# Two heads in 32 array columns: the value product of a pruned attention kernel

## The reference

```python
q, k, v = heads(xn @ w_attn.T + b_attn)            # 16 heads of 8 columns
att = q @ k.T / sqrt(8), causal
S = relu(att[:, 0]), column 0 and diagonal set to 0  # head 0 only
FF = cumsum over the rows of S, shifted by one row
att = att - FF[:, None]
keep = the 102 smallest FF of a row (fewer in early rows), and the diagonal
att = where(keep, att, -inf)
y = softmax(att) @ v
out_attn = y @ w_proj.T + b_proj
# ffn: top 2 of 8 experts by a softmax gate; each expert relu(xn@wi.T + bi + lora) @ wo.T + bo
```

## Time and profile before

| what | us |
|---|---|
| median of 3 executions (660.19 to 662.8) | 660.26 |
| the profiled execution | 663.88 |
| its span, first to last instruction | 661.9 |
| busy: TensorE, VectorE, GpSimd, ScalarE | 561.8, 505.3, 445.7, 378.0 |
| one batch of 44 slots, undisturbed | 74.2 |
| start of the first score | 48.1 |
| mean granted clock of TensorE, share of full | 0.958 |

### The profile page before, as it was taken

One profiled execution on the slowest core, in us unless ns is written; L12 is line 12 of the kernel. 1 busy time (PEld: TensorE's weight loads), 2 busy tenths in 40 slices (PEclk: granted clock), 3 DMA queues, 4 the chain that ended last, 5 costly groups with the idle time before them and its releaser, 6 DMA issues.

```text
span 661.9 us, 16486 instructions
## 1 busy us (share of the span) xinstructions
PE 561.8 (85%) x5434; PEld 382.5 (58%) x5434; DVE 505.3 (76%) x1832; ACT 378.0 (57%) x815; POOL 445.7 (67%) x756
## 2 busy tenths in 40 slices
PE   4636879989888899889998898989998899899994
PEld 1413555766466665656566565666566565776583
DVE  7679798667997679857897769867897769975351
ACT  3452776565765565754756566664756556455542
POOL 7506948696578746796478955798478956496451
PEclk9656999999999899989999999999999999999998
DMA  4152052134001520025100430025000430000000
GB/s 100 25 63 27 1 63 35 30 47 61 1 17 28 65 30 1 18 47 63 11 18 17 60 45 1 17 43 70 9 1 18 60 44 1 2 14 5 1 2 17
DMA packets 30068, 19.56 MB, mean 30 GB/s; under 512 B 6089, under 2 KB 29856, under 8 KB 29984
## 3 DMA queue, kind: packets, MB, share of 16 engines
q1 hardware_dynamic: 29984, 18.50, 19.5%
HBM read 3.22 MB, written 2.10 MB: 8 GB/s over the span
## 4 chain that ended last, share of the span: by engine, by line
PE 41%; DVE 19%; POOL 15%; issue 11%; ACT 7%; SPq 4%; DMA 1%; DVEq 1%; ACTq 0%; POOLq 0%
PE ps_t L923 10%; POOL ar L549 9%; PE ps_o L942 9%; PE ps_s L910 6%; PE ps_m L855 4%; SPq L407 4%; DVE ar L1330 4%; ACT work L648 2%; PE ps_m L851 2%; DVE work L1150 2%; PE ps_m L867 2%; ACT pr L734 2%; POOL hsum L563 1%; PE ps_m L873 1%; PE ps_m L885 1%
## 5 line engine op out<-in xcount | busy, mean ns | idle before, releaser
L549 POOL TENSOR_SCALAR ar<-ar,mx 128x512 f32<-128x512 f32 (+3 forms) x512 | 280.2, 561 | 171.4 <-DVE mx L1330 165.1
L734 ACT ACTIVATE pr<-ps_t 128x512 f32<-128x512 f32 (+1 forms) x352 | 192.4, 558 | 80.9 <-PE ps_t L923 78.8
L1330 DVE CUSTOM_DVE_ANT_0 ar<-ps_s,mask 128x256 f32<-128x256 f32 (+2 forms) x384 | 202.9, 550 | 33.2 <-PE ps_s L910 32.3
L923 PE MATMUL ps_t<-ident,ar 128*128 128x128 f32 x1280 | 202.6, 277 | 16.5 <-POOL ar L549 11.0
L923 PEld LDWEIGHTS ps_t<-ident,ar 128*128 128x128 f32 x1280 | 156.2, 142 | 57.2 <-POOL ar L549 27.4
L910 PE MATMUL ps_s<-ks,qs 96*128 96x512 bf16 (+3 forms) x512 | 130.4, 307 | 11.7 <-DVE mx L1327 6.0
L942 PE MATMUL ps_o<-pr,va 128*32 128x128 f32 x2560 | 98.8, 282 | 7.6 <-ACT pr L734 6.1
L942 PEld LDWEIGHTS ps_o<-pr,va 128*32 128x32 f32 x2560 | 63.4, 111 | 48.5 <-ACT pr L734 31.2
L910 PEld LDWEIGHTS ps_s<-ks,qs 96*128 96x128 bf16 x512 | 43.1, 99 | 56.5 <-issue 27.1
L719 ACT ACTIVATE h<-ps_m,bi_col 128x512 f32<-128x512 f32 x64 | 43.9, 687 | 54.9 <-PE ps_m L855 54.2
L855 PE MATMUL ps_m<-zm,b_t 128*128 128x512 f32 x128 | 67.7, 610 | 8.7 <-ACT h L719 8.7
(11 more groups left out here) (227 smaller groups left out, 772.1 us busy)
## 6 DMA issues: line engine op xcount, KB each, us to landing
qs<-parts SPq DMA_DIRECT2D x42, 128.0 KB
ks<-parts SPq DMA_DIRECT2D x42, 128.0 KB
xs<-in_L_attn_x SPq DMA_DIRECT2D x8, 256.0 KB, 3.0
out<-res SPq DMA_DIRECT2D x8, 192.0 KB, 2.0
first_heads<-parts SPq DMA_DIRECT2D x72, 8.0 KB
qs<-parts SPq DMA_DIRECT2D x12, 64.0 KB
ks<-parts SPq DMA_DIRECT2D x12, 64.0 KB
out<-res SPq DMA_DIRECT2D x8, 64.0 KB, 10.5
```

The lines of the kernel that those rows point to most:

```text
L549: nc.gpsimd.tensor_scalar(col, col, -1.0, mx[:, t % NA_RING, j:j + 1], ALU.mult, ALU.add)\
L734: nc.scalar.activation(pr[:, u % NP_RING, 0:w], ps_t[u % NT_RING][:, 0:w], ACT.Exp, scale=-1.0)\
L923: last = nc.tensor.transpose(ps_t[u % NT_RING][:, P * j:P * j + P], ar[:, u % NA_RING, P * j:P * j + P], ident[:, :])
L1330: nc.vector.tensor_tensor_reduce(out=ar[:, t % NA_RING, w * j:w * j + w], in0=ps_s[t % NS_RING][:, w * j:w * j + w], in1=mask[:, k % 2, OF ...
```

## The change

The value product puts two heads into 32 array columns, 16 for each. va gets a layout by pairs of heads (PAIR = 41 columns: v of the even head and a one, filler, nine zeros, filler, v of the odd head and a one). The even head's matmul takes 32 columns from the start of the pair, so that its own rows are 0 to 8 and zeros fall on rows 16 to 24; the odd head's takes 32 columns from 16 on and is accumulated into the same place, its rows being 16 to 24. ORDER arranges the heads so that groups 0 and 1 (2 and 3) hold the even and the odd heads of the same pairs. A row block then needs 256 columns of ps_o, and two row blocks share the bank. out_t is copied at slots 16 and 48 only, ot and yt have two jobs per batch in place of four (at 19 and 50, 22 and 52), each for two row blocks, and proj0 and proj1 now take two row blocks each; their slots and all others stay. va is filled by four copies per v job, since even and odd heads and the two row blocks are copied apart, and GpSimd fills the zeros with eight more fills at the start. The tile s0 goes, and its data is kept in the tile work, so that its writer waits for masks of the batch before.

```diff
@@ -47,7 +47,10 @@
...
-OW = 512 // NH
+OW = 32
+HALF_OW = OW // 2
+PAIR = 41
+OUT_COLS = HALF_OW * NH
@@ -73,6 +76,8 @@
...
+ORDER = [8 * (i // 8) + 2 * (i % 4) + i % 8 // 4 for i in range(NH)]
@@ -89,8 +94,8 @@
...
-OT_AT, YT_AT, PROJ_AT = (12, 19, 36, 50), (17, 22, 39, 52), (40, 55)
-ATT_JOBS = [(f"ot{a}", OT_AT[a], "dve") for a in range(NA)] + [(f"yt{a}", YT_AT[a], "act") for a in range(NA)] + \
+OT_AT, YT_AT, PROJ_AT = (19, 50), (22, 52), (40, 55)
+ATT_JOBS = [(f"ot{a}", OT_AT[a], "dve") for a in range(2)] + [(f"yt{a}", YT_AT[a], "act") for a in range(2)] + \
@@ -244,11 +249,17 @@
...
-        va = sb("va", [P, 2, NA, (NH - 1) * VW + OW])
-        s0 = sb("s0", [P, FOFF[NA]])
+        va = sb("va", [P, 2, NA, NH // 2 * PAIR + VW])
...
+        s0_place = ((0, 0), (1, 0), (2, 0), (1, 3 * P))
+        def s0(j, lo, hi):
+            row, at = s0_place[j]
+            return work[:, row, at + lo:at + hi]
@@ -287,13 +298,13 @@
...
-        bias_part = hsum[0:1, 0:3, :].rearrange("o f t -> o (f t)").bitcast(BF16)[:, 0:6 * (NA - 1) * C]\
-            .rearrange("o (j q a c) -> o j q a c", j=2, q=3, a=NA - 1)
+        bias_part = hsum[0:1, 0:3, :].rearrange("o f t -> o (f t)").bitcast(BF16)[:, 0:12 * C]\
+            .rearrange("o (j q a c) -> o j q a c", j=2, q=3, a=2)
...
-        rec = sb("rec", [P, NH])
+        rec = sb("rec", [P, 2 * NH])
@@ -475,6 +486,8 @@
...
+                    for p in range(NH // 2):
+                        link(nc.gpsimd.memset(va[:, :, :, PAIR * p + HALF_OW:PAIR * p + HALF_OW + VW], 0.0))
@@ -689,11 +702,11 @@
...
-                                    act.wait_ge(scanned, NA * (n - 1) + j + 1)
+                                    act.wait_ge(mask_done, NA * (n - 1) + s0_place[j][0] + 1)
...
-                                nc.scalar.activation(s0[:, FOFF[j]:FOFF[j] + w], m[:, 0:w], ACT.Relu,
+                                nc.scalar.activation(s0(j, 0, w), m[:, 0:w], ACT.Relu,
@@ -703,8 +716,12 @@
...
-                                copy(va[:, into(n), both, 0:NH * VW].rearrange("p a (h d) -> p a h d", d=VW)[:, :, :, 0:HD],
-                                     m3[:, :, 0:P].rearrange("p a (h d) -> p a h d", d=HD), name, n, False)
+                                for i, a in enumerate(half):
+                                    for s in range(2):
+                                        copy(va[:, into(n), a, 0:NH // 2 * PAIR]
+                                             .rearrange("p (h d) -> p h d", d=PAIR)[:, :, OW * s:OW * s + HD],
+                                             m3[:, i, 0:P].rearrange("p (h s d) -> p h s d", s=2, d=HD)[:, :, s, :],
+                                             name, n, False)
@@ -720,9 +737,9 @@
...
-                                if n >= 1 and a in (0, 3):
-                                    wait_full(act, ("proj0", "proj1")[a == 3], n - 1)
-                                copy(yt[:, a, :], m[:, 0:P], name, n)
+                                if n >= 1:
+                                    wait_full(act, f"proj{a}", n - 1)
+                                copy(yt[:, 2 * a:2 * a + 2, :].rearrange("p a t -> p (a t)"), m[:, 0:2 * P], name, n)
@@ -734,12 +751,12 @@
...
-                            for a in range(NA):
+                            for a in (1, 3):
...
-                                    if NA * kk + a >= 1:
-                                        wait_full(act, f"ot{(a + 3) % NA}", kk - (a < 1))
+                                    if 2 * kk + a // 2 >= 1:
+                                        wait_full(act, f"ot{1 - a // 2}", kk - (a < 2))
@@ -861,26 +878,28 @@
...
-                                             bias_rows[:, 1, 0:hi - lo, :].rearrange("p a c -> p (a c)"), start=True, stop=False)
+                                             bias_rows[:, 1, :, :].rearrange("p a c -> p (a c)"), start=True, stop=False)
...
-                            pe.wait_ge(taken, NA * n + a + 1)
-                            for c in range(GROUPS):
+                            pe.wait_ge(taken, 2 * n + a + 1)
+                            for c in range(4):
...
-                            last = nc.tensor.transpose(m[:, 0:P], y[:, a, :, :].rearrange("p h d -> p (h d)"), ident[:, :])
+                            for i in range(2):
+                                last = nc.tensor.transpose(m[:, P * i:P * i + P],
+                                                           y[:, 2 * a + i, :, :].rearrange("p h d -> p (h d)"), ident[:, :])
...
-                            lo, hi = ((0, NA - 1), (NA - 1, NA))[int(name[4])]
-                            wait_read(pe, f"yt{hi - 1}", n)
+                            lo, hi = ((0, 2), (2, NA))[int(name[4])]
+                            wait_read(pe, f"yt{lo // 2}", n)
...
-                                             bias_rows[:, 0, 0:hi - lo, :].rearrange("p a c -> p (a c)"), start=True, stop=False)
+                                             bias_rows[:, 0, :, :].rearrange("p a c -> p (a c)"), start=True, stop=False)
@@ -907,8 +926,8 @@
...
-                            last = nc.tensor.matmul(ps_s[u % NS_RING][:, w * j:w * j + w], qs[:, k % 2, h0 + j, P * a:P * a + P],
-                                                    ks[:, k % 2, h0 + j, 0:w], start=True, stop=True)
+                            last = nc.tensor.matmul(ps_s[u % NS_RING][:, w * j:w * j + w], qs[:, k % 2, ORDER[h0 + j], P * a:P * a + P],
+                                                    ks[:, k % 2, ORDER[h0 + j], 0:w], start=True, stop=True)
@@ -929,20 +948,23 @@
...
-                        if group == 0 and NA * k + a >= 1:
-                            pe.wait_ge(taken, NA * k + a)
-                        elif group == 0:
+                        if group == 0 and a % 2 == 0 and 2 * k + a // 2 >= 1:
+                            pe.wait_ge(taken, 2 * k + a // 2)
+                        elif group == 0 and a == 0:
...
+                        block, odd = divmod(group, 2)
+                        col = OUT_COLS * (a % 2) + P * block
...
-                                last = nc.tensor.matmul(ps_o[OW * j:OW * j + OW, P * group:P * group + P],
-                                                        va[:, k % 2, c, VW * hh:VW * hh + OW],
+                                from_v = PAIR * (ORDER[hh] // 2) + HALF_OW * odd
+                                last = nc.tensor.matmul(ps_o[OW * j:OW * j + OW, col:col + P],
+                                                        va[:, k % 2, c, from_v:from_v + OW],
...
-                                                        start=(c == 0), stop=(c == a))
+                                                        start=(c == 0 and odd == 0), stop=(c == a and odd == 1))
@@ -997,7 +1019,7 @@
...
-                        for a in range(1, NA - 1):
+                        for a in range(1, 2):
@@ -1288,15 +1310,15 @@
...
-                                o3 = m[:, :].rearrange("p (h d) -> p h d", d=OW)
-                                link(nc.vector.reciprocal(rec[:, :].rearrange("p (h o) -> p h o", o=1),
-                                                          o3[:, :, HD:VW]))
+                                o4 = m[:, :].rearrange("p (g d) -> p g d", d=HALF_OW)
+                                link(nc.vector.reciprocal(rec[:, :].rearrange("p (g o) -> p g o", o=1),
+                                                          o4[:, :, HD:VW]))
...
-                                    y[:, a, :, :], o3[:, :, 0:HD],
-                                    rec[:, :].rearrange("p (h o) -> p h o", o=1).to_broadcast([P, NH, HD]), ALU.mult)\
+                                    y[:, 2 * a:2 * a + 2, :, :].rearrange("p a h d -> p (a h) d"), o4[:, :, 0:HD],
+                                    rec[:, :].rearrange("p (g o) -> p g o", o=1).to_broadcast([P, 2 * NH, HD]), ALU.mult)\
...
-                                lo, hi = ((0, NA - 1), (NA - 1, NA))[int(name[4])]
+                                lo, hi = ((0, 2), (2, NA))[int(name[4])]
...

```

8 lines of the change are left out of this document (4 added, 4 removed).

## The result

| | before | after |
|---|---|---|
| median of 12 executions | 660.23 | 665.47 |
| all executions | 656.8 to 664.6 | 662.2 to 668.5 |
| profiled execution, span | 663.88, 661.9 | 666.23, 664.5 |
| first score | 48.1 | 49.0 |
| last score to the end | 15.3 | 17.2 |

Of 255 executions whose clock is on record here, four were more than 1.5% longer than the fastest of their kernel, with a lower clock; they are left out of every comparison. The ratio is 1.0071 [1.0039, 1.0104]; a second measurement of the same kernel, a_again, gave 1.0069 [1.004, 1.0098]. The changed kernel is 0.7% slower. The time lies in the range of 656.0 to 666.0, but 3.4 us above the forecast of 662.1, and on the side to which I had given 0.28.

The account below looks back on a forecast made before the run. No engine is full; the lead changes by slot among TensorE, VectorE, GpSimd and ScalarE. Start +2.0, batch 0 -0.40, batches 1 to 5 +0.25, batch 6 -0.16, batch 7 -0.76, end +1.0: together +1.9, median 662.1 us, range 656.0 to 666.0.

Parts of the forecast that it names:

- Slot 36: Four transposes leave the chain at slot 36, and all of it passes into the GpSimd stretch: 0.44 us saved per batch.
- Slots 11 to 14: Transposes leave slot 12, but longer proj1 (+0.28) and four va copies (+0.11 per job) delay TensorE: +0.34 us per batch.
- Slot 19: Reciprocal of 32 columns and product of 256 on VectorE, in the chain: about +0.15 us, 0.02 of it the reciprocal.
- At slot 6 the same +0.15 is covered: The wider reciprocal and product at slot 6 cost nothing, as the second scan waits for GpSimd until 524.26.
- Batch 0: -0.44 at slot 36, -0.11 for slot 17's transpose, +0.15: -0.40 us; its v copies stand beside GpSimd.
- Batches 6 and 7: Batch 6 -0.16 us, as VectorE loses a reciprocal and product at slot 36; batch 7, led by TensorE, -0.76.
- The start: va's larger fills delay the first root by 2.3 us; less 0.35 for a bias copy, plus 0.1: +2.0, bounds 0 and +3.
- The end: After the last product, a chain of longer single steps, from reciprocal and product to a 128 KB store: +1.0 us.
- The clock: Rival, 0.16: one more stretch at 1.2 instead of 2.4 GHz, as TensorE gets more gaps; about +2.4 us, 664.5.
- the transposes count in full: Rival, 0.15: TensorE gives back 16 x 0.44 = 7.0 us, start and end take 3.0: 656.2 us.
- The slow copies: Rival, 0.12: small va copies at slots 11 and 13 do not overlap, 0.88 us instead of 0.29; 5.8 more: 667.9.
- the hidden start: Rival, 0.17: VectorE's four-column start instruction is slow by itself, or the first root not late: 659.8 us.

Follow-up runs that it names:

- b_fill: Kernel before, with score matmuls of slots 3, 7, 8 and 9 of batches 1 to 6 computed three times: 659.85 us, ratio 0.9993.
- b_v4: Kernel before, with the copies filling va split into four of 64 columns per v job, nothing else: 661.97 us, ratio 1.0014.
- b_half: Kernel before, with output jobs of row blocks 0 and 2 left out, those of 1 and 3 projected in their place: 654.95 us, ratio 0.9912.
- a_slots: Kernel after, with out_t transposes moved from slot 19 to 30, y transposes from 22 to 35, second projection from 11 to 26: 667.47 us, ratio 1.0091.
- b_proj: Kernel before, with projection jobs, stores and bias rows cut into two row blocks each instead of three and one: 664.89 us, ratio 1.0052.
- a_fill: Kernel after, with score matmuls of slots 3, 7, 8 and 9 of batches 1 to 6 computed three times: 661.14 us, ratio 1.0000 to before.
- a_start: Kernel after, with va's fills moved on GpSimd from ahead of the first root to after batch 0's q and k: 661.31 us, ratio 0.9992 to before.
- a_v2: Kernel after, with va filled by two copies of 128 columns per v job instead of four of 64: 665.30 us, ratio 1.0083 to before.
- b_busy: Kernel before, with scores of slots 2, 3, 6 to 9, 36 and 37 computed two or three times in all batches: 665.04 us, ratio 1.0075.

## Why the prediction was right or wrong

To hold the terms against measurements, undisturbed stretches have to be compared, and each is taken from a run in which it is undisturbed. The two profiles of after agree within 0.02 us on the three that are undisturbed in both (batches 1 and 2, and 7 to its last score). View by windows, a_again, batches 1 to 5 and the stretch after the last score:

```profile
134.67:209.12 74.45, 65.65 (x669) 45.04 (x668) 60.43 (x220) 45.00 (x101) 54.71 (x93) 1.00 0.21 31
209.12:284.04 74.92, 65.64 (x669) 45.03 (x668) 59.75 (x220) 45.11 (x101) 54.51 (x93) 1.00 0.22 31
284.04:358.67 74.63, 65.66 (x669) 45.04 (x668) 60.15 (x220) 45.01 (x101) 54.53 (x93) 1.00 0.22 31
358.67:433.66 74.99, 65.66 (x669) 45.03 (x668) 60.12 (x220) 44.99 (x101) 54.53 (x93) 1.00 0.22 31
433.66:508.26 74.60, 65.64 (x669) 45.04 (x668) 60.10 (x220) 45.01 (x101) 54.50 (x93) 1.00 0.22 28
...
644.17:660.80 16.63, 7.21 (x99) 5.01 (x97) 2.43 (x7) 4.70 (x9) 2.04 (x3) 0.82 0.03 9
```

And b_fill, batches 2, 3, 6 and 7, which before has disturbed (in 7 nothing is repeated):

```profile
209.20:283.81 74.61, 67.95 (x696) 47.49 (x695) 60.67 (x224) 45.82 (x99) 54.68 (x93) 1.00 0.23 31
283.81:357.95 74.14, 68.08 (x696) 47.50 (x695) 60.55 (x224) 45.90 (x99) 54.66 (x93) 1.00 0.23 31
...
506.89:577.86 70.97, 65.33 (x688) 46.73 (x687) 58.78 (x215) 40.72 (x88) 48.70 (x85) 1.00 0.21 29
577.86:640.63 62.77, 59.86 (x639) 42.09 (x638) 34.49 (x119) 32.18 (x63) 40.78 (x73) 1.00 0.02 6
```

| part | forecast | measured |
|---|---|---|
| first score | +2.0 | +0.9 |
| batch 0 | -0.4 | +0.1 |
| batches 1 to 5 | +0.25 | +0.3 to +1.5 |
| batches 6 and 7 | -0.9 | -0.6 (133.1 against 133.7) |
| after the last score | +1.0 | +1.3 to +1.9 |
| sum | +1.9 | +2.0 to +3.8 |
| lower clock | none | +1.3 |

Batches 1 and 5, undisturbed in before itself, are +0.23 and +0.38; batch 4 is +0.10, with the pause of 0.65 in before. The five together are 373.6 us in a_again and 372.1 in before, if its batches 2 and 3 are taken from b_fill. But there TensorE's wait for the first-head transfers at slot 4 is short (1.39 and 1.12 us); in before itself it is 2.14 and 2.10, and in b_v4, which has neither repeats nor a stretch, 2.12 and 2.32. With b_v4's two batches, less its 0.18 for the copies, before is at 373.3, and the difference is +0.3.

- **Slot 36: right.** The score of slot 37 comes 0.44 us earlier in batch 1 of after, and 0.44 in b_half; forecast 0.44.
- **Slots 11 to 14: right in kind, short in size.** A place where work is removed got slower, by 0.45 us from slot 10 to slot 15 instead of 0.34. The mis-sized term is the copies, 0.15 per job and not 0.11. The estimate from the page "Perfetto Trace Analysis", section "Optimizing Scalar/DVE Operations", of the Trainium skill was 0.15, and the measurement agrees with it rather than with my line through three sizes.
- **Slot 19: right in place, short in size.** VectorE's timeline of after, batch 5:

```profile
475.76 0.35 DVE L1314 RECIPROCAL rec<-ps_m 128x32 f32<-128x32 f32 x1
476.14 0.42 DVE L1316 TENSOR_TENSOR y<-ps_m,rec 128x256 f32<-128x256 f32 x1
```

  The reciprocal is 0.09 longer than in the earlier trace rows, not 0.02, and the product 0.13; together 0.22. Against before, batch 5, VectorE's list in a_again is 0.60 us late up to the reciprocal, 0.83 behind the product, and stays 0.83 late. TensorE's scores, which run ahead of it, show the same 0.24 only at slot 28. In a_slots, where the job has left slot 19, the score of slot 28 comes 0.6 us earlier by comparison, and in b_half, b_v4 and b_proj, with the old sizes, nothing changes there.
- **"At slot 6 the same +0.15 is covered": right.** It shows as 0.22 at slot 9, and is gone at slot 10: a_again reaches slot 10 of batches 4 and 5 at 17.28 us, b_proj, with the narrow reciprocal and product, that of batches 1 and 4 at 17.26 and 17.27. What I had left out are the transfers: proj0 is shorter, they start earlier, and TensorE's wait for them at slot 4 falls from 1.51 to 1.15 us in batch 5. By slot 10 the 0.40 gained is gone again, and the score is between 0.05 earlier (batch 1) and 0.15 later (batch 5) than before. With 0.11 more at slots 11 to 15 and 0.08 more at slot 19 than forecast, this is the difference between +0.05 and the measured +0.23 and +0.38.
- **Batch 0: wrong.** The score of slot 15 comes 0.5 us later. The four copies are not what does it: b_half, with one copy per v job, has the same 0.5 there, and b_v4, with four, 0.2. It comes with the jobs that are gone, and how is open.
- **Batches 6 and 7: right.** -0.6 for -0.9. The profile before has a stretch of lower clock in slot 40 of batch 6, so that its own batch 7 (62.27 us) is no reference (b_v4, undisturbed there, has b_fill's time for batch 7); the 0.3 us were not taken apart.
- **The start: right up to the root, wrong behind it.** minus_mean at 8.80 and L1000's end at 17.74 were forecast as 8.7 and 17.6, the first score as near 50, and it came at 48.99. The step that failed is the bias copy. I subtracted 0.35, which is what the copy that stays takes; what goes is 1.68 less 0.35, and with the shorter fill of the bias rows b_proj measures 1.5 at the next instruction. 2.4 less 1.5 is the measured +0.9. With this slip put right the forecast would have been about 661, over 4 us below the result: that it was off by no more than 3.4 is partly luck, since the term counted too high stood in for the clock, which was counted as nothing.
- **The end: right in kind, short in size.** Timeline of all engines, after:

```profile
655.33 0.36 DVE L1314 RECIPROCAL rec<-ps_m 128x32 f32<-128x32 f32 x1 [6.80 <-PE ps_m L890]
655.72 0.42 DVE L1316 TENSOR_TENSOR y<-ps_m,rec 128x256 f32<-128x256 f32 x1
...
657.43 1.06 PE L904 MATMUL ps_m<-wp_t,yt 128*128 128x128 f32 x4
658.53 0.42 DVE L1326 TENSOR_TENSOR res<-ps_m,down 128x256 f32<-128x256 f32 x1 [2.39 <-PE ps_m L904]
```

  The four matmuls of the last projection take 1.06 us here, at a granted clock of 0.50 (1.2 GHz), and 0.61 in slot 40 of batch 5, at 1.00. TensorE waits for single steps at the end, with 7.21 us of work in the last 16.63, and the clock had fallen by then. I had taken the prices of full clock.
- **The clock: the step that failed in the sum.** I held a further stretch at the lower clock for a rival at 0.16, beside the forecast, and priced it at 2.4 us. What came is both together: at equal clock the change costs about 3 us, more than forecast, and the clock adds 1.3. The step was to treat the lower clock as one stretch that comes or not. It is an average over executions: after has 2 to 4 us more at the lower level, and a single profile of it shows between none (a_again, batches 1 to 5) and three. That TensorE's idling is what lowers it is borne out by a_fill and not by b_fill.
- **The rivals.** That the transposes count in full fell with the slots of b_half (0.44 at slot 37, but 0.20 of 0.44 at slots 10 to 13), not with its total of 5.8 us, whose interval holds the 7.0. The slow copies fell with the starts in ScalarE's timeline (0.43 us for four copies, not 0.88), the hidden start with L1000's 5.42 us.

## What to carry to other kernels

Halving operations beside the bound is worth what the slots let through, here 0.6 to 0.9 us per batch of the 1.6 us that TensorE had less to do, and is easily eaten by what comes with it at places that do count: constants ahead of the first root, small copies ahead of an exponential, a longer tail of single steps. Work out those first, since they were also the ones that could be repaired (a_start, a_v2). When an instruction goes, subtract what goes and not what stays. And before a place is called a new loss, look whether it is an old one arriving late: TensorE runs ahead of VectorE by some slots, and showed at slot 28 what had been lost at slot 19. When an engine with a clock that is granted gets less to do, compare the time at the lower clock over all executions, not in one profile, before explaining a difference of half a per cent by instructions.

## What the runs showed of the hardware

- One stretch of 3.4 us at 1.2 GHz costs 1.4 to 1.7 us of a batch here; the wait ahead of it can make the batch longer still (2.3 in before, 3.5 in b_half). Over 251 executions 1 us at the lower level goes with 0.32 us of time. Work repeated into the same bank ahead of such places left no stretch in batches 1 to 5 of the profiles; it made after 4 us faster (665.2 to 661.1) and before not at all (659.75 and 659.85).
- TensorE can pause inside a group of matmuls with nothing that it waits for in the profile: 0.39 us idle and the batch 0.65 longer in before, 0.93 in a_fill, 2.70 in b_busy. No two of these stand at the same matmul; the cause is open.
- A VectorE instruction of four columns took 3.04 us and then 5.42, held both times to the end of a GpSimd fill that shares no data with it, the second time from inside one fill to the end of the next.
- A reciprocal from PSUM takes 0.26 us for 16 columns and 0.35 for 32: 0.09 for 16 columns more, where the product takes 0.13 for 128 more.
- Left open: why a_fill has less low time than b_fill (44.1 against 49.8 us) with the same repeats, what brings 0.5 us at slot 15 of batch 0, why the first-head transfers land up to 2.3 us later in one batch than in another, and why emptying slot 11 in a_slots did not keep the clock.
